# Last attention units of a four-stage transformer kernel: who divides the last weights, and when the next stage's pieces are issued

## The reference, cut to what matters

```python
x = x + _L1_xattn_ref(_layernorm(x, axis=-1), ctx_1024, mask_BxS_ik0, ...)   # stage C
x = x + _L1_ffn_ref(_layernorm(x, axis=-1), ...)                            # stage D
...
def _L1_ffn_ref(x, Win, bin_, W1, b1, W2, b2, Wout, bout):
    s = jnp.einsum('btd,dm->btm', x, Win) + bin_
    h = jax.nn.relu(s[..., None] * W1 + b1)          # 16 inner values for each of 64 m
    g = jnp.einsum('btmh,mh->btm', h, W2) + b2
    out = jnp.einsum('btm,md->btd', g, Wout) + bout
    return out
```

## Time and profile before

| | us |
|---|---|
| median of 3 runs | 355.14 |
| lowest and highest | 354.05 and 356.2 |
| the profiled execution, its own time | 355.5 |
| its span in the trace | 353.5 |
| mean granted TensorE clock, share of full | 0.986 |

### The profile page before, as it was taken

The page is one execution under the profiler, slowest core; times in us unless marked ns, Lnnn a source line. Parts: engine busy times, 40 slices in busy tenths (PEclk is TensorE's granted clock), DMA queues, the critical chain, the costliest instruction groups (busy, mean ns, idle before and its releaser), DMA issues.

```text
span 353.5 us, 6757 instructions
## 1 busy us (share of the span) xinstructions
PE 320.7 (91%) x2375; PEld 228.9 (65%) x2375; DVE 242.0 (68%) x608; ACT 216.0 (61%) x633; POOL 118.9 (34%) x150
## 2 busy tenths in 40 slices
PE   7787999998899898979998999987899999999696
PEld 2245887664566544425544998985487778878684
DVE  5977766594899877752632563277778967888576
ACT  1568886164237364555777754744558576676995
POOL 3434563101510033330531350410567535445400
PEclk9998999999999999999999999999899999999999
DMA  7680000056877100019002003101000000000002
GB/s 218 205 239 2 2 0 2 6 177 200 210 238 220 41 2 0 2 21 342 4 15 69 0 24 93 53 0 43 10 17 16 2 0 2 1 3 0 0 2 60
DMA packets 21590, 22.44 MB, mean 63 GB/s; under 512 B 3606, under 2 KB 18358, under 8 KB 21558
## 3 DMA queue, kind: packets, MB, share of 16 engines
q1 hardware_dynamic: 19750, 19.93, 19.3%
q0 software_dynamic: 512, 1.05, 1.0%
q10 hardware_dynamic: 1296, 1.05, 0.9%
HBM read 14.22 MB, written 7.60 MB: 62 GB/s over the span
## 4 chain that ended last, share of the span: by engine, by line
PE 55%; DVE 24%; ACT 10%; issue 4%; DMA 3%; POOL 2%; SPq 0%; ACTq 0%; DVEq 0%; POOLq 0%
PE PS L1276 47%; DVE mB L814 9%; PE PS L1324 6%; ACT big L1086 4%; ACT big L1252 2%; DVE big L673 2%; DMA big<-in_A_WkT 1%; ACT big L1204 1%; DVE big L635 1%; DVE XN L618 1%; DVE mraw L627 1%; DMA scr_y<-big 1%; ACT big L1060 1%; DVE U L618 1%; DVE stats L607 1%
## 5 line engine op out<-in xcount | busy, mean ns | idle before, releaser
L1276 PE MATMUL PS<-big 128*128 128x128 f32 (+10 forms) x592 | 96.6, 315 | 10.1 <-DVE big L635 2.7
L1276 PEld LDWEIGHTS PS<-big 128*128 128x128 f32 (+3 forms) x592 | 59.0, 154 | 44.0 <-issue 14.3
L507 POOL TENSOR_TENSOR big<-big,urec 128x1024 f32<-128x1024 f32 x24 | 45.6, 1900 | 63.7 <-DVE urec L666 45.2
L1086 ACT ACTIVATE big<-big 128x154 f32<-128x154 f32 x192 | 60.4, 319 | 8.4 <-DVE big L673 6.7
L1204 ACT ACTIVATE big<-PS 128x1024 f32<-128x1024 f32 (+3 forms) x64 | 42.2, 706 | 24.7 <-PE PS L1276 24.4
L814 DVE TENSOR_REDUCE mB<-PS 128x2 f32<-128x256 f32 (+5 forms) x90 | 50.1, 622 | 7.1 <-PE PS L1276 7.1
L1060 ACT ACTIVATE big<-PS 128x1280 f32<-128x1280 f32 (+2 forms) x30 | 32.7, 1092 | 35.0 <-PE PS L1324 32.6
L1276 PE MATMUL PS<-kkC,XT 128*128 128x462 f32 (+1 forms) x96 | 37.9, 532 | 3.4 <-DVE big L673 3.4
L1276 PE MATMUL PS<-cstb 128*128 128x128 bf16 x192 | 37.9, 219 | 0.0
L1086 ACT ACTIVATION_READ_ACCUMULATOR big<-big 128x1 f32 x192 | 36.4, 189 | 0.0
L495 POOL TENSOR_TENSOR rstd<-ve,minus_half 128x4 f32<-128x4 f32 (+2 forms) x13 | 13.2, 1017 | 68.2 <-DVE ve L613 68.2
(11 more groups left out here) (187 smaller groups left out, 477.1 us busy)
## 6 DMA issues: line engine op xcount, KB each, us to landing
scr_qk<-big SPq DMA_DIRECT2D x12, 384.0 KB, 3.8
big<-scr_qk SPq DMA_DIRECT2D x16, 288.0 KB
big<-in_wv SPq DMA_DIRECT2D x1, 2048.0 KB, 8.2
scr_x<-zrow SPq DMA_DIRECT2D x2, 448.0 KB, 6.4
scr_y<-big SPq DMA_DIRECT2D x2, 448.0 KB, 3.6
X<-in_x ACTq DMA_DIRECT2D x2, 256.0 KB, 3.6
big<-in_A_WoT ACTq DMA_DIRECT2D x1, 512.0 KB, 4.6
cw<-in_C_Wk SPq DMA_DIRECT2D x1, 512.0 KB, 5.1
```

The lines of the kernel that those rows point to most:

```text
L507: pool.tensor_tensor(pn[:, 0:GH * P].rearrange("p (h k) -> p h k", h=GH), Pt[u % 3][:, :, 0:KM], r.to_broadcast([P, GH, KM]), ALU.mult).th ...
L1086: i = act.activation(Pt[u % 3][:, h, :], Pt[u % 3][:, h, :], ACT.Exp, accum_out=usum[:, u % 3, h:h + 1])
L1276: return pe.matmul(o, lhsT, rhs, start=start, stop=stop)
```

## The change

It has four pieces. The division of the last unit's weights is shared: POOL takes heads 0 to 4, DVE heads 5 to 7 and the 26 remaining keys of all heads. The first part's norm, turning, copy and inner input are each issued one loop step earlier on DVE, PE and ACT. Around the last two units PE and ACT run their pieces in another order. DVE sums j = 5 to 7 of part 0 after the last tile has been added rather than before.

```diff
@@ constants
-        J_FIRST = 2
-        J_EARLY1 = 6
-        J_EARLY = 4
-        J_LATE = 7
-        J_DIRECT = 3
+        J_ADD = 5
+        H_LAST = 5
-        U_LNC, U_LND = 2 * QT - 1, 2 * QT + 6
+        U_LNC, U_LND = 2 * QT - 1, 2 * QT + 5
@@ POOL, unit_norms
+                    if st == "C" and u == UNITS["C"] - 1:
+                        pool.tensor_tensor(pn[:, 0:H_LAST * P].rearrange("p (h k) -> p h k", h=H_LAST),
+                                           Pt[u % 3][:, 0:H_LAST, 0:KM], r[:, 0:H_LAST].to_broadcast([P, H_LAST, KM]),
+                                           ALU.mult).then_inc(unit_norm[st], 1)
+                        continue
@@ DVE
+            def normalise_last():
...
+                dve.wait_ge(unit_rec["C"], u + 1)
+                dve.wait_ge(unit_turned["C"], u - 1)
+                dve.tensor_tensor(pn[:, H_LAST * P:GH * P].rearrange("p (h k) -> p h k", h=GH - H_LAST),
+                                  Pt[u % 3][:, H_LAST:GH, 0:KM], r[:, H_LAST:GH].to_broadcast([P, GH - H_LAST, KM]),
+                                  ALU.mult).then_inc(norm_last, 1)
+                dve.tensor_tensor(pn[:, GH * P:BLK * P].rearrange("p (h k) -> p h k", h=GH)[:, :, 0:KR],
+                                  Pt[u % 3][:, :, KM:KEYS], r.to_broadcast([P, GH, KR]), ALU.mult).then_inc(norm_last, 1)
             def ln_d_first():
-                ln_apply("d", X, XN, 0)
...
-                2 * QT + 5: ln_d_first})
+                2 * QT + 4: lambda: ln_apply("d", X, XN, 0),
+                2 * QT + 5: ln_d_first,
+                2 * NT: normalise_last})
...
-            sum_inner(0, range(1))
+            sum_inner(0, range(2))
             ln_apply("d", X, XN, 1, PARTS[1])
-            sum_inner(0, range(1, GH))
+            sum_inner(0, range(2, J_ADD))
             add_tile("C", NT - 1)
             ln_stats("d", X, 2, lambda: dve.wait_ge(tile_added["C"], NT), PARTS[2])
+            sum_inner(0, range(J_ADD, J_ADD + 1))
             ln_apply("d", X, XN, 2, PARTS[2])
+            sum_inner(0, range(J_ADD + 1, GH))
@@ ACT
-                inner_units(0, range(J_FIRST))
+                inner_units(0, range(1))
-                        2 * NT - 1: first_inner, 2 * NT: lambda: inner_units(0, range(J_FIRST, J_EARLY))})
+                        U_LND + 1: first_inner, U_LND + 2: lambda: inner_units(0, range(1, 3)),
+                        U_LND + 3: lambda: inner_units(0, range(3, 4))})
+            inner_units(0, range(4, 6))
             ln_d_out(1)
-            inner_units(0, range(J_EARLY, J_LATE))
+            inner_units(0, range(6, 7))
             inner_input(1)
-            inner_units(0, range(J_LATE, GH))
-            inner_units(1, range(J_EARLY1))
+            inner_units(0, range(7, GH))
+            inner_units(1, range(5))
             ln_d_out(2)
-            inner_units(1, range(J_EARLY1, GH - 1))
+            inner_units(1, range(5, 6))
             inner_input(2)
-            inner_units(1, range(GH - 1, GH))
+            inner_units(1, range(6, GH))
@@ PE, weigh_values: called back after 4 of the 10 blocks
+                    if midway and k == GH // 2:
+                        midway()
@@ PE, turn_weights
+                if st == "C" and v == UNITS["C"] - 1:
+                    pe.wait_ge(unit_norm[st], 2 * v + 1)
+                    pe.wait_ge(norm_last, 2)
@@ PE, units_C
                     if u == n_u + 1:
                         turn_weights("C", u - 2)
+                        weigh_values("C", u - 3, vwm, vwr)
                         turn_d(1)
-                        weigh_values("C", u - 3, vwm, vwr)
-                        inner_input(1)
+                        continue
+                    if u == n_u + 2:
+                        weigh_values("C", u - 3, vwm, vwr, lambda: inner_input(1))
                         continue
...
-                2 * NT - 1: lambda: inner_input(0)},
+                U_LND + 1: lambda: inner_input(0)},
...
+            pe.wait_ge(ww_ready, GH)
+            direct_outputs(1, range(1))
+            turn_d(2)
+            direct_outputs(1, range(1, 3))
+            inner_input(2)
             last_outputs(0)
-            pe.wait_ge(ww_ready, GH)
-            direct_outputs(1, range(J_DIRECT))
-            turn_d(2)
-            inner_input(2)
-            direct_outputs(1, range(J_DIRECT, GH))
+            direct_outputs(1, range(3, GH))
```

More of the change, by code:

```diff
@@ L339, in program @@
             "s_in_mm", "s_in_ready", "relu_ready", "ffn_mm", "ffn_added"))
+        norm_last = sem("norm_last")
         stored = sem("stored")
@@ L999, in ln_c_second @@
                 x_plus(1, rowv[:, R_BOUT1, :])
+            def normalise_last():
+                u = UNITS["C"] - 1
+                r = urec[:, u % 3, :].unsqueeze(2)
+                pn = PN[u % 2]
+                dve.wait_ge(unit_rec["C"], u + 1)
[5 more added lines that the diff above has]
+                                  Pt[u % 3][:, :, KM:KEYS], r.to_broadcast([P, GH, KR]), ALU.mult).then_inc(norm_last, 1)
             def ln_d_first():
-                ln_apply("d", X, XN, 0)
                 dve.wait_ge(ln_norm["d"], QT)
@@ L1292, in turn, with weigh_values @@
                     i.then_inc(ln_turned[name], 1)
-            def weigh_values(st, v, vwm, vwr):
+            def weigh_values(st, v, vwm, vwr, midway=None):
                 per = PER[st]
@@ L1314, in turn_weights @@
             def turn_weights(st, v):
-                pe.wait_ge(unit_norm[st], 2 * v + 2)
+                if st == "C" and v == UNITS["C"] - 1:
+                    pe.wait_ge(unit_norm[st], 2 * v + 1)
+                    pe.wait_ge(norm_last, 2)
+                else:
+                    pe.wait_ge(unit_norm[st], 2 * v + 2)
                 if v >= 1:
```

## The result

The changed kernel was timed three times, each time beside the kernel before. Each ratio, with its 95% interval, is formed from fast executions alone (a slow one lies more than 1.5% above the fastest of its kernel) and is not the quotient of the medians beside it, which are over all executions: in the first row, where all eight were fast, that quotient is 1.0105.

The account below looks back on a forecast made before the run. PE was taken to bound the stage until 326.56 us, DVE's late sums its end: sums ending at 352.1 plus 0.4 at the port, plus 3.34, give 355.84 us span, +2.34, so 357.5 us median; range 355.3 to 358.4.

Parts of the forecast that it names:

- Step 4: PE from the last turning on: same work, other order, same clock; values of unit 15 end at 342.5 us, before 342.07.
- Step 1: First part one loop step sooner: PE's values behind tile 4 +0.24 us, exponentials of unit 15 1.1 us later.
- Step 2: ACT's new order around the last units: 0.6 of 1.1 us comes back, turning of unit 15 starts +0.5 us.
- Step 3: Last unit's division shared by POOL and DVE: 1.3 us side by side, 2.2 in turn; no gain, no loss.
- the clock stays up: Rival at PE's wait ahead of the last turning: no clock fall, last values 1.7 us sooner, 355.8 us; chance 0.18.
- Step 5: DVE behind the last tile: late sums and join add 2.93 us, 0.66 fills a wait; sums end at 352.1 us.
- Step 6: SBUF port shared by DVE's sum and POOL's power: a delay of 0 to 0.72 us, taken as 0.4.

Follow-up runs that it names:

- POOL alone: Changed kernel with the last unit's division wholly on POOL again, all else as changed: 359.14 us, ratio 1.0083 to the kernel before.
- the last experiment: Kernel before with only the shared division of the last unit's weights added: 357.3 us, ratio 1.001.
- First part back: Changed kernel with the first part's norm, turning and inner input back at their old loop steps: 358.06 us, ratio 1.0065 to the kernel before.
- the clock held up late: Changed kernel with matmuls that nobody reads in PE's three waits near the end: 357.17 us, ratio 1.003 to the kernel before.
- before, sums late: Kernel before with DVE's sums of j = 5 to 7 behind the last tile's addition and PE's last outputs later: 359.28 us, ratio 1.0089.
- changed, again: Changed kernel without an edit, timed a second time: 357.5 us, ratio 1.0054 to the kernel before.
- sums back: Changed kernel with DVE's sums of j = 5 to 7 and the join ahead of the last tile's addition again: 357.2 us, ratio 1.0042.

## Why the prediction was off, point by point

The direction was right, and the ratio over all three measurements, 1.0066, is the forecast's (2.34 us of 355.14). That it fits so well is luck: two terms of the sum were wrong with opposite signs. The first measurement, 359.1 us, lies 0.7 above the range, the third 0.6 above, and the second, 357.5, on the forecast. Two things failed. Step 4 had the clock wrong, and that made the forecast too late, not too early. What carried the time above the range came, as far as the traces show, from outside the stage, for which the sum had no term.

**Step 1** held. `XT,win` stands ahead of the last scores without idle time, PE's values behind tile 4 start 0.13 us later (+5.71 against +5.58; forecast 0.24), and the exponentials of unit 15 end at +25.14 against +24.08, 1.06 later (forecast 1.1). **Step 2** held: the turning starts at +27.80, 0.34 later (forecast 0.5), released by ACT's copy.

**Step 3**, the shared division worth nothing, held for the release: 0.08 us between POOL alone and shared. The two engines did not work side by side at full speed. POOL's 640 elements took 1.63 us where 1.26 was reckoned, DVE's 208 took 1.43 where 0.37 was, and the whole was done in 1.90 us (332.78 to 334.68), between the forecast's 1.3 (side by side) and 2.2 (by turns). The rule of the Trainium skill, "SBUF — State Buffer", Who interferes with whom, by which one of two such instructions is held for the other's length, agrees: DVE's piece ends 0.23 us behind POOL's. That the cost on DVE is covered is right for the changed order (the last tile waits for PE, 1.82 us), but not for the old one (the last experiment).

**Step 4 is the step that failed**: "the same work follows in another order, at the same clock". The clock did not stay as it was. It no longer fell in the last turning, in any of the seven profiles with the early first part, and the last tile was added at +34.56, 1.3 us sooner than before, not 0.4 later. The rival "the clock stays up" had this mechanism and its size (last values 1.7 us before the forecast's +36.3), and I gave it 0.18. "First part back" brings back wait and fall, and filling the wait in the kernel before gives most of the gain (0.93 us at the last tile) without moving anything; so it is PE's wait ahead of the turning that matters. It does not decide every time: with 2.25 us the clock fell in three profiles of four.

**Step 5 had its mechanism right and was 0.65 us short.** Behind the last tile the forecast had 7.29 - 0.66 + 2.93 + 0.4 = 9.96 us, and with the clock held up late 9.93 were measured. In the changed kernel it was 10.61. What the step left out is the effect on PE: with the last outputs moved behind the late sums, PE has nothing to fill its waits for ACT's relu and the norm (0.87, 1.25) and gets a third, for the sums (1.07). In all seven profiles in which the sums were late and nothing filled these waits, "before, sums late" among them, the clock fell at +37 to +42. Which of the waits does it isn't shown: the fall came ahead of the wait for the sums in four of the seven ("changed, again" at +38.1, that wait beginning at +38.4), in it in two (the first and third profile of the changed kernel), behind it in one ("before, sums late"). And "sums back" had 0.87 and 2.00 us and no fall. So the fall was not removed, but moved from +28 to about +38 in the changed kernel, where DVE waits for PE's last outputs. The rival's 355.8 us failed on this: its last addition was due at +45.7 (1.7 us before the forecast's +47.4), and with the late waits filled it did come at +45.73. **Step 6**, 0.4 us at the port, measured 0.45 (1.00 against 0.55).

The errors of steps 4 and 5 partly cancel: the last tile came 1.75 us before the forecast's time and the way behind it took 0.65 longer, so the sums end at +45.2, where +46.3 was forecast. Of the signs named in the prediction, the release by ACT and the exponentials held. DVE's idle time ahead of the last tile was 1.82 us, not over 2.5, and the last matmuls waited for DVE in the first profile alone, not in the second and third. The clock at full after 334 us and the last tile before 341 us (341.94, less the 1.14 from before the stage, is 340.8) were signs of being wrong, and both came. The top of the range was also added up wrong: 0.72 at the port and 0.3 for the division give 358.1, not 358.4.

**The term that was missing.** The forecast's last addition was due at +47.4, and it came at +46.40, +47.01 and +47.25, 1.4 to 2.2 us behind the +45.03 of before. The stage thus accounts for most of the 2.4 us, and in no profile for more than was forecast. The 359.1 us of the first measurement need more than the stage. In its profiled execution that is 1.14 us from before the stage; the three others have no trace. For half-clock stretches and late inputs outside the changed stage I had put no term into the range. The four executions had mean granted clocks of 0.966 to 0.981. Among the executions of the kernel before in each of the three larger sets, 0.01 less clock went with 1.3 to 2.3 us more time, so such scatter can cover the 1.6 us between the first and the second measurement; that it did isn't shown, and in the second measurement itself clock and time did not go together. Why the changed kernel had the lower clock on average in both later measurements too (0.983 against 0.986, 0.976 against 0.984) is only partly explained: a late fall twice as long as the old one (from 343.0 to 349.8 us in the third profile, 334.1 to 337.5 before) accounts for 3.4 us of half clock, about 0.005 of the span, and the rest stays open.

## What to carry to other kernels

A wait of PE has two prices, the idle time and what the clock does behind it; a change that shortens one wait and lengthens another can move the slow stretch, and it must be looked for at the new place. Work moved behind the last input of an in-order engine is paid there, less what fills a wait (here 2.64 us of 2.93: 9.93 with PE kept busy against 7.29 before), however idle that engine was ahead of it. And four runs don't fix a median to 0.5% here (359.1, 357.5 and 358.98 us of one kernel): repeat the kernel before explaining what is left over.

## What was not expected of the hardware

The same wait had two outcomes: behind 2.25 us without work PE's clock fell to 1.2 GHz in three profiles and stayed at 2.4 GHz in a fourth, whose PE did the same instructions up to there. Shorter waits close together did it too: in "changed, again" the clock fell 1.0 us after the second of two waits, 0.87 and 1.25 us, while in "sums back" it stayed up behind 0.87 and 2.00 us. So the length of the waits alone does not tell whether it falls. And 1.0 us of matmuls that nobody reads, four of them, could stand in a wait without delaying what followed by more than 0.01 us (the last outputs start at +39.43 against +39.42).
